# First stage of a two-layer transformer kernel: projections of the feed-forward part moved next to the normalisation of queries and keys, their product given to GpSimd

## The chip, the cores and the metric

The kernel runs on one core of a Trainium2 chip. The core has a matrix engine (TensorE, PE in the profile, with its weight loads shown as PEld), a vector engine (VectorE, DVE), a scalar engine (ScalarE, ACT), GpSimd (POOL) and SyncE (SP), which here only issues transfers. The engines run their own instruction streams and meet at semaphores. The metric is the device time of one execution in microseconds, as the median of several; lower is better.

## The reference, cut to what matters

Two transformer layers over one sequence of 2048 tokens of width 128, everything in float32:

```
xn = layernorm(x)
x = x + attn0(xn) + ffn0(xn)           # layer 0
xn = layernorm(x)
x = x + attn1(xn) + ffn1(xn)           # layer 1

attn0: q, k, v = split(xn @ w_qkv.T + b_qkv); 16 heads of 8 dims
       q = q / |q|, k = k / |k|        # norm of each head's 8 numbers
       score = (1 + arccos(q.k)) ** -3.2, scaled by row and column sums, rows normalised
       out = probs @ v @ w_out.T + b_out
ffn0:  gate = xn @ (w_gate/127).T; up = xn @ (w_up/127).T      # 384 columns each
       out = (silu(gate) * up) @ (w_down/127).T                # back to 128
```

The change touches only the stage that computes the first layernorm, q, k and v, the norms of q and k, and all of ffn0.

## The kernel before

The program runs stage after stage, each a block of five instruction streams that ends with all engines meeting: `stage_project0` (this change), `stage_attention0` (16 heads), `stage_project1`, `stage_attention1`, `stage_output`. Within a stage the order on each engine is the order in which the code is written; nothing reorders it.

`stage_project0` holds the 2048 tokens as 16 tiles of 128 (NT = 16) or as four chunks of 512 columns (NCH = 4), and the 384 hidden columns of ffn0 as three tiles of 128 (M0 = 3), so that gate and up have 12 pieces each, of 128x512, numbered k.

- **TensorE** turns the normalised x (L245), multiplies it with the weights of q, k, v (L252), then does gate and up piece by piece (L261 into `psG`, L263 into `psU`, two PSUM banks each, k % 2). Piece k waits for the product of piece k - 2. After all twelve it turns q and k, split into three bfloat16 parts (L271, 96 transposes into `psT`), and at last does the down projection (L279, 16 tiles of three matmuls into `psQ`).
- **VectorE** does layernorm, adds the bias to q, k and v, and then works on q and k as one array of 128x4096: squares (L174, into the array `two`), sums in groups of 8 (L176), waits for a square root from ScalarE, one Newton step and the reciprocal (L178 to L183 on 128x512), the scaling (L186, `qkn_ready`), and the split into three bfloat16 parts (L189 to L192, `parts_ready`). Only after that come its twelve products of gate and up (L198, one input in PSUM, one in SBUF) and its sixteen additions of down and x into `base` (L203).
- **ScalarE** copies the turned x, takes the square root of the norms (L224), does twelve Silu (L229 into `sil`, two buffers), then copies twelve pieces of turned parts from PSUM (L233 into `stg`).
- **GpSimd** waits for `qkn_ready`, and makes the products of pairs of q and of k that head 0 needs (`products`: a copy at L287, eight multiplications at L294; `factors`: L305 to L312).
- **SyncE** stores six pieces of `stg` as they come (L127), waits for them, waits for all of `base`, stores it (L131) and waits for that store.

The stage ends when every engine has come to its end. `stage_attention0` uses the memory of `base` as a scratch array (`folds`, first written by VectorE at L527, some way into head 0) and loads `base` again at its end.

Of the kernel before, what the change touches and what calls it, by code (L numbers as in the profile page):

```python
# [6 lines left out]
ALU = mybir.AluOpType  # L7
# [21 lines left out]
KST = NPART * NPART * HD0  # L29
GEXP = -3.2  # L30
# [29 lines left out]
def stage_project0(nc, io, sb):  # L60
# [3 lines left out]
    with ExitStack() as ctx:  # L64
# [29 lines left out]
        sil = t("sil0", [P, 2, BANK])  # L94
# [13 lines left out]
        gate_ps, up_ps, sil_ready, h_ready = sem("gate_ps0"), sem("up_ps0"), sem("sil_ready0"), sem("h_ready0")  # L108
        pt_ps, pt_ready, parts_stored = sem("pt_ps"), sem("pt_ready"), sem("parts_stored")
        down_ps, base_ready, base_stored = sem("down_ps0"), sem("base_ready0"), sem("base_stored")  # L110
        qkn_ready, mono, mono_ready = sem("qkn_ready"), sb["mono"], sb["mono_ready"]
        psTb = psT[:, :, :].rearrange("p a b -> p (a b)").bitcast(BF16).rearrange("p (a b) -> p a b", a=2)

        with nc.Block() as block:
            @block.sync
            def _(sp):
# [7 lines left out]
                for i in range(NPART):  # L124
                    for x in range(2):
                        sp.wait_ge(pt_ready, 2 * (2 * i + x) + 2)
                        sp.dma_start(io["parts"][i, x].rearrange("h d t -> (h d) t"), stg[:, i, x, :])\  # L127
                          .then_inc(parts_stored, 16)
                sp.wait_ge(parts_stored, 16 * 2 * NPART)
                sp.wait_ge(base_ready, NT)  # L130
                sp.dma_start(io["base"], base[:, :, :].rearrange("p n d -> p (n d)")).then_inc(base_stored, 16)  # L131
                sp.wait_ge(base_stored, 16)

            @block.vector
            def _(eng):
# [53 lines left out]
                link(eng.tensor_copy(parts[:, 0, :, :], qkn[:, :, :]))  # L189
                link(eng.tensor_tensor(qk[:, :, :], qkn[:, :, :], parts[:, 0, :, :], ALU.subtract))  # L190
                link(eng.tensor_copy(parts[:, 1, :, :], qk[:, :, :]))
                eng.tensor_tensor(parts[:, 2, :, :], qk[:, :, :], parts[:, 1, :, :], ALU.subtract)\  # L192
                   .then_inc(parts_ready, 1)
                for k in range(NCH * M0):
                    n_, m = k // M0, k % M0
                    eng.wait_ge(up_ps, k + 1)
                    eng.wait_ge(sil_ready, k + 1)
                    eng.scalar_tensor_tensor(out=hT[:, m, n_ * BANK:(n_ + 1) * BANK], in0=psU[:, k % 2, :],  # L198
                                             scalar=DEQ, in1=sil[:, k % 2, :], op0=ALU.mult,
                                             op1=ALU.mult).then_inc(h_ready, 1)  # L200
                for k in range(NT):
                    eng.wait_ge(down_ps, k + 1)
                    eng.scalar_tensor_tensor(out=base[:, k, :], in0=psQ[:, k % 2, 0:D], scalar=DEQ,  # L203
                                             in1=x_in[:, k, :], op0=ALU.mult, op1=ALU.add).then_inc(base_ready, 1)

            @block.gpsimd
            def _(eng):
                fac = sb["fac"]
                for i, f in enumerate(F_ROWS):
                    eng.memset(fac[:, 0, :, 3 * NMON + i:3 * NMON + i + 1], GQK * GQK)  # L210
                    eng.memset(fac[:, 1, :, 3 * NMON + i:3 * NMON + i + 1], -f * GQK * GQK)
                eng.wait_ge(qkn_ready, 1)
# [4 lines left out]
            def _(eng):  # L217
# [5 lines left out]
                eng.wait_ge(n2_ready, 1)  # L223
                eng.activation(nrm[:, :], n2[:, :], ACT.Sqrt).then_inc(nrm_ready, 1)  # L224
                for k in range(NCH * M0):
                    eng.wait_ge(gate_ps, k + 1)
                    if k >= 2:
                        eng.wait_ge(h_ready, k - 1)
                    eng.activation(sil[:, k % 2, :], psG[:, k % 2, :], ACT.Silu, scale=DEQ).then_inc(sil_ready, 1)  # L229
                for k in range(2 * NPART * 2):  # L230
# [6 lines left out]
            def _(eng):  # L237
# [17 lines left out]
                for k in range(NCH * M0):  # L255
                    n_, m = k // M0, k % M0
                    rhs = xnT[:, n_ * BANK:(n_ + 1) * BANK]
                    if k >= 2:
                        eng.wait_ge(sil_ready, k - 1)
                        eng.wait_ge(h_ready, k - 1)  # L260
# [4 lines left out]
                eng.wait_ge(parts_ready, 1)  # L265
                for k in range(2 * NPART * 2):
# [1411 lines left out]
```

## Time and profile before

| | |
|---|---|
| median of 3 runs | 3647.53 us (3646.39 to 3648.2) |
| the profiled execution | 3644.35 us, its span 3642.6 us |
| busy shares of the span | PE 86%, ACT 83%, DVE 77%, POOL 73% |
| first stage | up to 116.07 us after the span's start |
| layer 0's attention | from there to about 1940 us |

The profile is of one execution. Its rows tell for a line, an engine and an operation how many instructions there were, how long they took and what ended the idle time before them. In the timeline a row starts with the start in microseconds and the duration of the group of instructions; of a group of several, the duration runs from the start of the first to the end of the last. A tile name stands for the memory and not for the variable: `two` is the array that the code of the first stage calls `qkn`.

### The profile page before, as it was taken

To read this page: it belongs to the slowest core of one execution; us is meant where nothing else is said; L and a number is where in the kernel's file an instruction comes from. 1 tells how busy PE (TensorE), PEld (TensorE's weight loads), DVE (VectorE), ACT (ScalarE), POOL (GpSimd) and SP (SyncE) were. 2 spreads that over 40 slices of the span, in tenths; PEclk is the share of its full clock that TensorE was granted. 3 is DMA by queue.
4 is the path that set the end of the run, shared out by engine and by line. 5 is a ranking of instruction groups with operands and counts; after the bars stand their busy time and mean duration, and the time that the engine had idled before them with its cause. 6 is when DMAs were issued, how large, how long until landed. Compare 5 with 4: busy or idle time off the path is not lost. (4 is left out here: it accounts for less than half of the span.)

```text
span 3642.6 us, 59779 instructions
## 1 busy us (share of the span) xinstructions
PE 3123.6 (86%) x19264; PEld 1306.7 (36%) x19264; DVE 2800.0 (77%) x3981; ACT 3013.6 (83%) x2658; POOL 2666.2 (73%) x1450
## 2 busy tenths in 40 slices
PE   4888888888889888898886968888888888888899
PEld 2322222222222122221222424555555555555547
DVE  7678988889888898888987977787877778787301
ACT  1799999999999999999995846887878878788722
POOL 2698988989889898898973525776777777677600
PEclk8876677766777667776676978999999999999999
DMA  0100000000000000000001450110001110000100
GB/s 23 53 7 7 0 7 7 6 7 0 6 7 6 6 0 6 7 6 6 0 10 38 140 163 25 42 30 25 24 25 34 34 30 24 25 24 27 38 0 12
DMA packets 59508, 85.46 MB, mean 23 GB/s; under 512 B 9808, under 2 KB 45904, under 8 KB 58960
## 3 DMA queue, kind: packets, MB, share of 16 engines
q1 hardware_dynamic: 59344, 83.06, 8.1%
q8 instruction: 129, 2.11, 0.2%
q14 instruction: 35, 0.29, 0.0%
HBM read 52.44 MB, written 30.54 MB: 23 GB/s over the span
## 5 line engine op out<-in xcount | busy, mean ns | idle before, releaser
L1195 POOL TENSOR_TENSOR lo<-pr,hi 128x1024 f16<-128x1024 f32 x384 | 917.3, 2413 | 384.5 <-ACT hi L1321 382.5
L1244 DVE TENSOR_REDUCE mx<-mx_ps 128x1 f32<-128x512 f32 x1024 | 659.8, 683 | 165.3 <-PE mx_ps L1359 161.8
L1336 ACT ACTIVATE pr<-s_ps 128x1024 f32<-128x1024 f32 x512 | 532.3, 1040 | 264.4 <-PE s_ps L1380 235.2
L1321 ACT ACTIVATE hi<-pr 128x1024 f16<-128x1024 f32 x512 | 548.2, 1072 | 0.0
L1359 PE MATMUL mx_ps<-ka,qa 128*128 128x512 f16 x1024 | 385.8, 398 | 141.5 <-DVE mx L1244 116.9
L671 ACT ACTIVATE wt<-wt 128x2048 f32<-128x2048 f32 x256 | 485.0, 1896 | 0.5
L477 POOL TENSOR_TENSOR wt<-base,wt 128x1024 f32<-128x1024 f32 x192 | 459.1, 2391 | 15.1
L662 ACT ACTIVATE wt<-wt,theta_bias 128x10240 f32<-128x10240 f32 (+2 forms) x96 | 464.3, 4837 | 0.9
L1399 PE MATMUL pv_ps<-vh,hi 128*128 128x129 f16 x4096 | 432.9, 222 | 11.2 <-ACT sums L1327 5.8
L1378 PE MATMUL s_ps<-qa,ka 128*128 128x512 f16 x1024 | 396.7, 387 | 35.1 <-issue 22.4
L473 POOL TENSOR_TENSOR base<-base,shift 128x1024 f32<-128x1024 f32 x192 | 364.1, 1897 | 83.7 <-DVE base L527 83.7
L1399 PE MATMUL pv_ps<-vh,lo 128*128 128x65 f16 x4096 | 418.6, 194 | 0.0
L1380 PE MATMUL s_ps<-qb,kb 65*128 65x512 f16 x1024 | 397.7, 388 | 0.0
L1399 PEld LDWEIGHTS pv_ps<-vh,hi 128*128 128x128 f16 x4096 | 372.8, 98 | 62.4 <-POOL lo L1195 11.1
L477 POOL TENSOR_TENSOR wt<-vb,wt 128x1024 f32<-128x1024 f32 x160 | 379.2, 2370 | 12.6
L1399 PEld LDWEIGHTS pv_ps<-vh,lo 128*128 128x128 f16 x4096 | 366.4, 99 | 55.7 <-issue 3.3
L750 PE MATMUL m_ps<-mst 110*128 110x512 f16 (+1 forms) x640 | 321.2, 609 | 47.5 <-ACT wt L651 19.6
L643 ACT ACTIVATE wt<-m_ps 128x1024 f32<-128x1024 f32 x352 | 332.9, 1032 | 24.8 <-PE m_ps L719 23.2
L473 POOL TENSOR_TENSOR vb<-vb,shift 128x1024 f32<-128x1024 f32 x160 | 303.4, 1897 | 60.1 <-DVE vb L527 60.1
L750 PE MATMUL r_ps<-mst 111*128 111x512 f16 (+1 forms) x768 | 314.5, 445 | 35.0 <-DVE wt L515 10.2
L1195 DVE TENSOR_TENSOR lo<-pr,hi 128x1024 f16<-128x1024 f32 x128 | 261.7, 2045 | 86.9 <-ACT hi L1321 86.9
L719 PE MATMUL m_ps<-mst 109*128 109x512 f16 x1024 | 307.6, 385 | 21.6 <-ACT wt L643 10.7
(196 smaller groups left out, 5265.4 us busy)
## 6 DMA issues: line engine op xcount, KB each, us to landing
qk<-stg SPq DMA_DIRECT2D x6, 2048.0 KB, 11.0
vh<-v SPq DMA_DIRECT2D x16, 520.0 KB, 3.5
qa<-qk SPq DMA_DIRECT2D x16, 512.0 KB, 3.6
ka<-qk SPq DMA_DIRECT2D x32, 256.0 KB, 4.7
v<-v_st SPq DMA_DIRECT2D x3, 2080.0 KB, 8.0
qst<-parts_dram SPq DMA_DIRECT2D x144, 32.0 KB
kst<-parts_dram SPq DMA_DIRECT2D x144, 32.0 KB
qk<-stg SPq DMA_DIRECT2D x4, 1024.0 KB, 8.2
```

What stands on the lines that cost most here:

```text
L473: eng.tensor_tensor(v, v, shift[:, 0:1].to_broadcast([P, 2 * BANK]), ALU.subtract)\
L477: eng.tensor_tensor(u, v, u, ALU.mult).then_inc(cubic, 1)
L662: eng.activation(wt[:, k:k + many, :], wt[:, k:k + many, :], ACT.Ln, bias=theta_bias[:, 0:1], scale=-2.0 if k >= NQ else -KA / (G4 * G4 * ...
L671: eng.activation(wt[:, k, :], wt[:, k, :], ACT.Exp, scale=GEXP, accum_out=n_c[:, k:k + 1])\
L750: mm = eng.matmul(slot(r)[:, cols(i, BANK)], mst[0:rows, 1, cols(k)], mst[0:rows, 0, rhs], start=True, stop=True)
L1195: eng.tensor_tensor(lo[:, i % NHL, :, :], pr_slot(i), hi[:, i % NHL, :, :], ALU.subtract).then_inc(lo_done, 1)
L1244: eng.tensor_reduce(mx4[:, q // NCH, q % NCH:q % NCH + 1], mx_ps[:, q % 2, :], AX.X, ALU.max)\
L1321: eng.activation(hi[:, i % NHL, :, :], pr_slot(i), ACT.Copy).then_inc(hi_done, 1)
L1336: eng.activation(pr_slot(i), s_ps[:, i % 2, :, :], ACT.Exp, scale=SM).then_inc(exp_done, 1)
L1378: eng.matmul(s_ps[:, i % 2, n_, :], ka[:, par, k * P:(k + 1) * P], qa[:, par, w], start=True, stop=False)
L1380: mm = eng.matmul(s_ps[:, i % 2, n_, :], kb[0:HD1 + 1, par, k * P:(k + 1) * P], qb[0:HD1 + 1, par, w], start=False, stop=True)
L1399: mm = eng.matmul(pv_ps[:, j // 2, j % 2 * OW:j % 2 * OW + cols], half[:, i % NHL, n_, j * P:(j + 1) * P], vh[:, par, k, 0:cols], start=(k ...
```

## The change

Five things change, all but the last in `stage_project0`.

- ScalarE now copies the up projection out of PSUM too, scaled, into a new buffer `up` (right behind each Silu), and a piece of PSUM is free for TensorE as soon as that copy is done (`up_taken`), not when the product is.
- The twelve products of gate and up go from VectorE to GpSimd, ahead of GpSimd's work on head 0. Both inputs are then in SBUF.
- ScalarE's square root of the norms comes behind four of the twelve pieces (NRM = 4).
- TensorE does the first half of down, turns the first part of q and k, does the second half of down, and turns the other two parts. VectorE announces each part for itself. Down goes into `psG` and `psU`, four token tiles to a bank, and VectorE adds x to four tiles with one instruction.
- SyncE issues the store of `base` ahead of its wait for the six part stores and doesn't wait for the store of `base` in this stage. VectorE waits for it (`base_stored`) in `stage_attention0` before its head 0.

```diff
@@ SyncE
-                sp.wait_ge(parts_stored, 16 * 2 * NPART)
-                sp.wait_ge(base_ready, NT)
+                sp.wait_ge(base_ready, NCH)
                 sp.dma_start(io["base"], base[:, :, :].rearrange("p n d -> p (n d)")).then_inc(base_stored, 16)
-                sp.wait_ge(base_stored, 16)
+                sp.wait_ge(parts_stored, 16 * 2 * NPART)
@@ VectorE
-                link(eng.tensor_copy(parts[:, 0, :, :], qkn[:, :, :]))
+                eng.tensor_copy(parts[:, 0, :, :], qkn[:, :, :]).then_inc(parts_ready, 1)
+                eng.wait_ge(parts_ready, 1)
...
-                for k in range(NCH * M0):
-                    n_, m = k // M0, k % M0
-                    eng.wait_ge(up_ps, k + 1)
-                    eng.wait_ge(sil_ready, k + 1)
-                    eng.scalar_tensor_tensor(out=hT[:, m, n_ * BANK:(n_ + 1) * BANK], in0=psU[:, k % 2, :],
-                                             scalar=DEQ, in1=sil[:, k % 2, :], op0=ALU.mult,
-                                             op1=ALU.mult).then_inc(h_ready, 1)
-                for k in range(NT):
-                    eng.wait_ge(down_ps, k + 1)
-                    eng.scalar_tensor_tensor(out=base[:, k, :], in0=psQ[:, k % 2, 0:D], scalar=DEQ,
-                                             in1=x_in[:, k, :], op0=ALU.mult, op1=ALU.add).then_inc(base_ready, 1)
+                for c in range(NCH):
+                    eng.wait_ge(down_ps, 4 * c + 4)
+                    four = slice(4 * c, 4 * c + 4)
+                    eng.scalar_tensor_tensor(out=base[:, four, :], in0=down(c).rearrange("p (n d) -> p n d", d=D),
+                                             scalar=DEQ, in1=x_in[:, four, :], op0=ALU.mult,
+                                             op1=ALU.add).then_inc(base_ready, 1)
@@ GpSimd
+                for k in range(NCH * M0):
+                    n_, m = k // M0, k % M0
+                    eng.wait_ge(up_taken, k + 1)
+                    eng.tensor_tensor(hT[:, m, n_ * BANK:(n_ + 1) * BANK], sil[:, k % 2, :], up[:, k % 2, :],
+                                      ALU.mult).then_inc(h_ready, 1)
                 eng.wait_ge(qkn_ready, 1)
@@ ScalarE
-                eng.wait_ge(n2_ready, 1)
-                eng.activation(nrm[:, :], n2[:, :], ACT.Sqrt).then_inc(nrm_ready, 1)
                 for k in range(NCH * M0):
+                    if k == NRM:
+                        eng.wait_ge(n2_ready, 1)
+                        eng.activation(nrm[:, :], n2[:, :], ACT.Sqrt).then_inc(nrm_ready, 1)
                     eng.wait_ge(gate_ps, k + 1)
                     if k >= 2:
                         eng.wait_ge(h_ready, k - 1)
                     eng.activation(sil[:, k % 2, :], psG[:, k % 2, :], ACT.Silu, scale=DEQ).then_inc(sil_ready, 1)
+                    eng.wait_ge(up_ps, k + 1)
+                    eng.activation(up[:, k % 2, :], psU[:, k % 2, :], ACT.Copy, scale=DEQ).then_inc(up_taken, 1)
@@ TensorE
                     if k >= 2:
-                        eng.wait_ge(sil_ready, k - 1)
-                        eng.wait_ge(h_ready, k - 1)
+                        eng.wait_ge(up_taken, k - 1)
...
+                for k in range(NT // 2):
+                    project_down(k)
+                turn_part(0)
+                for k in range(NT // 2, NT):
+                    project_down(k)
+                for i in range(1, NPART):
+                    turn_part(i)
@@ stage_attention0, VectorE
                 for x in range(2):
                     stack(0, x)
+                eng.wait_ge(sb["base_stored"], 16)
                 head(0, first=True)
```

TensorE, from the last piece of gate and up to the first matmul of the next stage. Before, all 96 transposes of the parts (L271) and then the 48 matmuls of down (L279):

```order
L261 MATMUL psG<-xnT,wg 128x512
L263 MATMUL psU<-xnT,wu 128x512
L271 MATMUL psT<-ident_b,parts 128x128 x96
L279 MATMUL psQ<-wd,hT 128x128 x48
L114 UNCONDITIONAL_BRANCH
```

And now, where `psG` and `psU` take the two halves of down:

```order
L270 MATMUL psG<-xnT,wg 128x512
L272 MATMUL psU<-xnT,wu 128x512
L293 MATMUL psG<-wd,hT 128x128 x24
L282 MATMUL psT<-ident_b,parts 128x128 x32
L293 MATMUL psU<-wd,hT 128x128 x24
L282 MATMUL psT<-ident_b,parts 128x128 x64
L120 UNCONDITIONAL_BRANCH
```

One third of the transposes now stands between the halves of down, and the other two thirds close the stage.

ScalarE, from the copies of turned x to the copies of turned parts. Before:

```order
L222 ACTIVATE xnT<-psT 128x512 x4
L224 ACTIVATE nrm<-n 128x512
L229 ACT_TABLE_LOAD
L229 ACTIVATE sil<-psG 128x512 x12
L233 ACTIVATE stg<-psT 128x1024 x12
```

And now, from the third of the four pieces ahead of the square root to the first behind it (a piece is a pair of L237 and L239):

```order
9 L237 ACTIVATE sil<-psG 128x512
10 L239 ACTIVATE up<-psU 128x512
11 L237 ACTIVATE sil<-psG 128x512
12 L239 ACTIVATE up<-psU 128x512
13 L233 ACT_TABLE_LOAD
14 L233 ACTIVATE nrm<-n 128x512
15 L237 ACT_TABLE_LOAD
16 L237 ACTIVATE sil<-psG 128x512
17 L239 ACTIVATE up<-psU 128x512
```

The square root moved behind four pieces, and there are two table loads more.

## Rows read from the trace of the kernel before

**Rows 1.** Busy time by stretch: start:end, length, then each engine; PEclk, DMA

```profile
42.00:70.00 28.00, 0.00 (x0) 0.00 (x0) 27.43 (x12) 2.56 (x4) 14.06 (x4) 0.50 0.00 0
70.00:74.00 4.00, 3.28 (x4) 1.51 (x5) 1.17 (x2) 0.60 (x1) 3.92 (x9) 0.50 0.00 0
74.00:90.00 16.00, 16.00 (x38) 6.94 (x37) 6.21 (x9) 5.39 (x9) 5.12 (x7) 0.98 0.00 1
```

**Rows 2.** Timeline of VectorE from 32 to 75 us: start, duration, engine, line

```profile
32.65 4.42 DVE L174 TENSOR_TENSOR two<-qk 128x4096 f32<-128x4096 f32 x1
37.11 4.42 DVE L176 TENSOR_REDUCE n<-two 128x512 f32<-128x4096 f32 x1
...
42.69 3.35 DVE L179 RECIPROCAL ntmp<-nrm 128x512 f32<-128x512 f32 x1
46.07 0.69 DVE L180 TENSOR_TENSOR ntmp<-ntmp,n 128x512 f32<-128x512 f32 x1
...
55.83 2.29 DVE L189 CAST parts<-two 128x4096 bf16<-128x4096 f32 x1
58.16 4.50 DVE L190 TENSOR_TENSOR qk<-two,parts 128x4096 f32<-128x4096 f32 x1
62.69 2.58 DVE L191 CAST parts<-qk 128x4096 bf16<-128x4096 f32 x1
65.31 4.67 DVE L192 TENSOR_TENSOR parts<-qk,parts 128x4096 bf16<-128x4096 f32 x1
```

**Rows 3.** Timeline of TensorE and ScalarE: projections, square root, turning, down

```profile
31.80 1.02 PE L261 MATMUL psG<-xnT,wg 128*128 128x512 f32 x2
41.56 0.63 ACT L224 ACTIVATE nrm<-n 128x512 f32<-128x512 f32 x1 [22.58 <-DVE n L176]
42.21 1.28 ACT L229 ACT_TABLE_LOAD   x1
81.37 1.02 PE L261 MATMUL psG<-xnT,wg 128*128 128x512 f32 x2
82.43 0.60 ACT L229 ACTIVATE sil<-psG 128x512 f32<-128x512 f32 x1 [1.12 <-PE psG L261]
90.60 11.11 ACT L233 ACTIVATE stg<-psT 128x1024 bf16<-128x1024 bf16 x12 [0.71 <-PE psT L271]
100.39 10.94 PE L279 MATMUL psQ<-wd,hT 128*128 128x128 f32 x96
```

**Rows 4.** DMA issues up to 125 us: KB each, median us to landing

```profile
parts_dram<-stg SPq DMA_DIRECT2D x6, 512.0 KB, 2.6
base_dram<-base SPq DMA_DIRECT2D x1, 1024.0 KB, 3.8
```

**Rows 5.** Timeline: issue of the store of base, next stage's first instruction

```profile
111.74 0.33 SPq L131 DMA_DIRECT2D base_dram<-base  x1
116.07 0.06 DVE L494 MEMSET theta_bias<- 128x1 f32 x1 [4.42 <-PEq L114]
```

**Rows 6.** Timeline of GpSimd: head 0's products, and head 1's at 117.25

```profile
55.86 2.52 POOL L287 COPY mono_x<-two 128x256 f32<-128x256 f32 x1 [54.59 <-DVE two L186]
58.46 13.67 POOL L294 TENSOR_TENSOR mono_p<-mono_x 128x256 f32<-128x256 f32 x8
77.94 1.25 POOL L312 TENSOR_TENSOR fac<-mono_p,fac 128x576 f16<-128x576 f32 x1
117.25 3.37 POOL L294 TENSOR_TENSOR mono_p<-mono_x 128x256 f32<-128x256 f32 x8
```

**Rows 7.** One line's instructions: duration in ns, min/median/max

```profile
L1066 POOL TENSOR_TENSOR hl<-ra,hl x64: 1154/1160/1167, 2001.5 to 2133.2; 128x512 f16<-128x512 f32 x64
L477 POOL TENSOR_TENSOR wt<-base,wt x192: 2361/2390/2427, 131.6 to 1941.8; 128x1024 f32<-128x1024 f32 x192
L1195 DVE TENSOR_TENSOR lo<-pr,hi x128: 1202/2096/2703, 2216.6 to 3432.9; 128x1024 f16<-128x1024 f32 x128
```

**Rows 8.** Busy time by stretch, layer 0's attention: columns as in rows 1

```profile
630.00:1030.00 400.00, 352.70 (x1306) 84.96 (x1308) 341.57 (x447) 393.14 (x275) 363.67 (x213) 0.70 0.02 5
```

## What the change does to the time: the prediction

> **What bounds the kernel now.** I first read busy time by stretch. From 42 to 70 us TensorE does nothing, ScalarE is busy for 2.6 us of 28, and VectorE is busy for 27.4 [rows 1]: one engine carries the stage. The timeline of VectorE says with what: squares, sums, reciprocals and the split of q and k, one behind the other from 32.65 to 69.98 us [rows 2]. Only then come gate and up (TensorE full from 74 to 90 [rows 1]), the turning of the parts (12 copies, 11.1 us), down (10.9 us) [rows 3] and the store of base, issued at 111.74 and landed 3.8 us later [rows 4, 5]. The next stage starts at 116.07 [rows 5], 0.53 us behind the landing. So the stage is two chains laid end to end: VectorE's, 70 us, and then 46 us of ffn0, turning and storing. None of the second needs VectorE's chain but the turning. Everything behind 116 us is the same work in both kernels, so what the stage loses in length the whole should lose.
>
> **The change part by part.** I follow each engine through the new order with durations of the old one.
>
> *Price of a piece.* In the old loop ScalarE's Silu lasts 0.60 us and starts 1.06 us after its matmul (81.37 to 82.43); with the 1.12 us that it waits for TensorE that is 1.72 us for a pair of gate and up, 0.86 each [rows 3]. The copy of up is the same shape from the same memory: 0.60. GpSimd's product of 128x512 isn't in this stage; its nearest rows are 1.16 us for 128x512 with a half-precision output, and 2.39 us for a float32 product of 128x1024, or 1.2 for half of it [rows 7]. I take 1.16, with 1.2 as the other end: 12 x 0.04 = 0.5 us at most, nothing below.
>
> *What VectorE and GpSimd do to each other.* GpSimd's small copy of 128x256 lasted 2.52 us from 55.86, until 0.26 us after VectorE's cast ended (58.12), and its eight multiplications of 3.37 us lasted 13.67 us beside L190 to L192 [rows 6, 2]. One GpSimd instruction gets through at each border between two VectorE instructions. The reverse holds too: VectorE's L191 is 0.29 us longer than its like L189, L192 0.25 longer than 4.42, and far later, beside GpSimd products of 2.1 us, VectorE's product L1195 has a median of 2096 ns against a least of 1202 [rows 2, 7]. But beside VectorE's instructions with one input in PSUM, GpSimd's L477 stays within 2361 to 2427 ns [rows 7]. So who has two inputs in SBUF, or is a cast, waits for GpSimd's running instruction and then holds it up. No row shows a sum (L176) or a reciprocal (L179, L183) beside GpSimd; they have one input, so I take them as free, and price the contrary below. L178 and L182 (tensor with scalar) I count with the casts. The Trainium skill (SBUF — State Buffer, section Who interferes with whom) has the same rule: an exclusive lock held for the whole instruction, and a tensor_reduce that never takes it on this chip; by it the time is the 3617 of the sum below, and without it for sum and reciprocals it is B's 3626. It speaks against this change only in that each product on GpSimd may hold VectorE up.
>
> *The walk.* Piece 0: matmuls from 31.80 [rows 3], Silu 32.86, copy done at 34.3. GpSimd is locked out by L174 until 37.07; product 0 ends at 38.25. Silu 2 waits for it, so products 1 to 3 follow at 1.2 us beside the sum L176 and end at 39.5, 40.8 and 42.05; ScalarE has copied piece 3 at 40.85. Its table load (1.28 [rows 3]) ends at 42.15, the square root at 42.8 instead of 42.19: VectorE **+0.6**. Another table load, then pieces 4 on, the first Silu at 44.15. Product 4 runs beside L179 and ends at 46.6. VectorE takes L180 at 46.7; L181 has to wait for product 5, **+1.15**; L182 for product 6, **+1.2**; products 7 to 9 run beside the reciprocal L183, and L186 waits for the rest of 9, **+0.2**. Product 10, shut out by L186 (54.5 to 58.95), delays L189 by **1.15**, and product 11 delays L190 by **1.15**. Sum 5.45: VectorE's chain ends at 69.98 + 5.45 = **75.4**. The last product is done at 63.6.
>
> *GpSimd behind it.* Its copy for head 0 now comes at the border of L190 and L191 and its first multiplication at the next; one border less than before is left, so beyond L192 it has the old rest (72.13 - 69.98 = 2.15) and one multiplication of 0.55 more, and then the factors, from 72.13 to 79.19 before = 7.06 [rows 6]. 75.4 + 2.7 + 7.06 = **85.2 us**. Before this was hidden (79.2 against 115.5); now it is the last thing in the stage.
>
> *TensorE, ScalarE and stores.* Gate and up are through by 57.6 (ScalarE gives a piece each 1.2 to 1.7 us behind TensorE), half of down takes 10.94 / 2 = 5.5 [rows 3] and ends at 63.1, part 0 (there since VectorE's cast, 62.4) is turned in 4 x 0.93 = 3.7 and done at 66.8, the other half of down at 72.3, part 1 (there at 70.6) at 76.0, part 2 (there at 75.4) at 79.7. Its store lands 2.6 us later [rows 4], 82.3, three before GpSimd. VectorE's four additions follow L192 and end at about 78.3. The store of base is issued behind the last part's, near 80, and lands at 84; VectorE asks for it only before head 0, eight us into the next stage: nothing, and if that cover went, 3.8 us at most. The two loads of tables are inside the walk. Sixteen additions become four: off the path. The next stage's stack loads (SyncE, ahead of nothing but themselves) shift with the stage.
>
> *Sum.* Next stage's first instruction: 85.2 + 0.5 = 85.7, against 116.07: **-30.4 us**. The profiled execution would be 3644.35 - 30.4 = 3614.0; the runs have a median 3.2 higher than it, so **3617.1 us**, a ratio of 0.9917.
>
> **The rivals.**
>
> *A. VectorE isn't held up by GpSimd* (it wins every border, or a product lets go early). Then its chain ends at 69.98 + 0.6, and GpSimd, if it has kept its place, at about 79.8: -35.8, **3611.7**. Against it stand the 2096 ns of L1195; for it, that the observed delays in this very stage are only 0.1 to 0.3 us, because the GpSimd instructions there were short.
>
> *B. Sum and reciprocals lock as well.* Every product then waits for a border. Walking it the same way, product 3 ends at 46.3, the square root at 47.0, one product of 1.2 goes into each of the borders up to L191, L192 ends at 83.8, and GpSimd at 83.8 + 3.4 + 7.06 = 94.3: -21.3, **3626**. This is also the case in which the change only half does what it says.
>
> *C. TensorE falls to its low clock.* With no matmul from 42 to 70 the granted clock was 0.50 (1.2 of 2.4 GHz), and stayed there for the first 4 us of work [rows 1]. Now TensorE works with gaps, in pieces paced by ScalarE and GpSimd. In layer 0's attention, also work with gaps, the granted clock is 0.70 on average with TensorE busy for 353 of 400 us [rows 8]. At 0.70 a pair takes 2.4 us: pieces 6 to 11 from 45.5 end at 60, half of down at 67.7, part 0 at 71.4, down at 79, parts 1 and 2 at 86.5, landed 89.2, stage end 89.7: -26.4, **3621**. At 0.50 all through (pairs 3.4, down 21.9) the same walk gives 102.1, or 3633.5. The Trainium skill (TensorE: Matmul & The Clock Gate, section A second HAM failure mode: psum-queue depth-cycling) describes a kernel in which short idles between groups of matmuls on PSUM banks make the clock go up and down: that is this rival. Against it: matmuls from 74 to 90 and the turning behind them had gaps and a full clock.
>
> *D. Slower than before.* Only the work behind the stage could eat 30 us, and there only ScalarE's stage of 16 heads is long enough (1826 us, 116.07 to 1941.8 [rows 5, 7]). There ScalarE is busy for 393 of 400 us and TensorE for 353 at a clock of 0.70 [rows 8]. TensorE becomes the bound when its clock falls under 0.70 x 353 / 400 = 0.62 on average, and from there each further 1% costs 18 us; 30 us are lost at 0.61. For that, a denser first stage would have to change what the chip grants over the next 1.8 ms. Price: **3648** or more. Nothing in the rows ties the two, since the clock in the attention stage starts from an idle gap of 5 us in both kernels.
>
> **How the numbers follow.** The walk as written: 55% (between 3613 and 3621, since each of five borders can fall the other way by about 1 us, and 1.16 or 1.2 us is open). A 15%, B 10%, C 15% (most of it near 3621), D 2%, and 3% for what I don't see, in either direction. The range from **3610 to 3627** takes in the walk, A, B and C at 0.70, and leaves out C at 0.50, D and the unseen. A change of 0.2% (7.3 us) is about what a measurement of this kernel can tell from none; all but D and part of the unseen lie beyond it: faster 96%, same 2%, slower 2%.
>
> **What the profile of the changed kernel would show.** The next stage's first memset at 84 to 88 us, with GpSimd's last factors (7 us of them, alone) ending half a microsecond before it and the part stores landed before. L174's like at 32.65 with the first product ending 1.2 us behind it; VectorE's small instructions between the two reciprocals 1.2 us apart more than before; casts and L186's like starting about 1 us late. The sum and the two reciprocals with products at 1.2 us inside them: if these are 3 to 4 us long, B holds. A granted clock near 1.0 from 45 to 80 us; near 0.5 or 0.7 with the last part store as the end of the stage, C. VectorE's chain ending by 71, A. The forecast is wrong altogether if layer 0's attention, from 116.07 to the start of the last L477 at 1941.8 [rows 7], isn't within 3 us of these 1825.7.

## The result, and the profile after

| | before | changed |
|---|---|---|
| median of the runs | 3646.96 us (3642.92 to 3648.2, 4 runs) | 3615.33 us (3613.58 to 3623.75, 4 runs) |
| ratio, 95% interval | | 0.9923 [0.9906, 0.9939] |
| the profiled execution, its span | 3644.35, 3642.6 us | 3623.75, 3621.9 us |
| next stage's first instruction | 116.07 us | 84.81 us |

The medians lie 31.6 us apart; the forecast was 30.4, and 3617.1 us for the median. The profiled execution of the changed kernel is the slowest of its four, which matters below.

The timeline of VectorE in the changed kernel, from the squares on, to be laid beside [rows 2]. A row starts with start and duration in microseconds:

```profile
32.62 4.42 DVE L179 TENSOR_TENSOR two<-qk 128x4096 f32<-128x4096 f32 x1
37.08 4.42 DVE L181 TENSOR_REDUCE n<-two 128x512 f32<-128x4096 f32 x1
42.56 0.43 DVE L183 TENSOR_SCALAR nrm<-nrm 128x512 f32<-128x512 f32 x1 [1.06 <-ACT nrm L233]
43.02 3.35 DVE L184 RECIPROCAL ntmp<-nrm 128x512 f32<-128x512 f32 x1
46.41 1.65 DVE L185 TENSOR_TENSOR ntmp<-ntmp,n 128x512 f32<-128x512 f32 x1
48.09 1.64 DVE L186 TENSOR_TENSOR ntmp<-ntmp,nrm 128x512 f32<-128x512 f32 x1
49.76 1.38 DVE L187 TENSOR_SCALAR ntmp<-ntmp 128x512 f32<-128x512 f32 x1
51.17 3.35 DVE L188 RECIPROCAL nrm<-ntmp 128x512 f32<-128x512 f32 x1
54.56 5.53 DVE L191 TENSOR_TENSOR two<-qk,nrm 128x4096 f32<-128x4096 f32 x1
60.12 3.24 DVE L194 CAST parts<-two 128x4096 bf16<-128x4096 f32 x1
63.40 4.50 DVE L196 TENSOR_TENSOR qk<-two,parts 128x4096 f32<-128x4096 f32 x1
...
70.56 4.66 DVE L199 TENSOR_TENSOR parts<-qk,parts 128x4096 bf16<-128x4096 f32 x1
```

The sum L181 and the two reciprocals last as long as before. L185, L186, L187, L191 and L194 are each 0.95 to 1.1 us longer than their likes before (0.69, 0.69, 0.43, 4.42, 2.29). With the root 0.37 us late that makes 5.3 us, and the chain ends at 75.22 instead of 69.98.

GpSimd in the same stretch, to be laid beside [rows 6]:

```profile
34.36 7.58 POOL L217 TENSOR_TENSOR hT<-sil,up 128x512 f32<-128x512 f32 x4 [33.09 <-ACT up L239]
45.00 2.50 POOL L217 TENSOR_TENSOR hT<-sil,up 128x512 f32<-128x512 f32 x2 [3.06 <-ACT up L239]
47.67 1.51 POOL L217 TENSOR_TENSOR hT<-sil,up 128x512 f32<-128x512 f32 x1 [0.17 <-ACT up L239]
49.39 1.47 POOL L217 TENSOR_TENSOR hT<-sil,up 128x512 f32<-128x512 f32 x1 [0.21 <-ACT up L239]
...
56.26 4.96 POOL L217 TENSOR_TENSOR hT<-sil,up 128x512 f32<-128x512 f32 x1 [0.45 <-ACT up L239]
61.17 2.46 POOL L309 COPY mono_x<-two 128x256 f32<-128x256 f32 x1
63.70 13.67 POOL L316 TENSOR_TENSOR mono_p<-mono_x 128x256 f32<-128x256 f32 x8
...
83.18 1.25 POOL L334 TENSOR_TENSOR fac<-mono_p,fac 128x576 f16<-128x576 f32 x1
```

The last product (56.26, 4.96 us) shows how the two engines shut each other out: it was ready before L191 ended, was held until it did (60.1), was through at 61.2, and L194 waited for it. GpSimd ends at 84.43, the next stage begins 0.38 us later. The part stores had landed before that: the last was issued at 80.1 and took 2.6 us, so 82.7.

What the rest gave back. Layer 0's attention took 1824.5 us by the count of the prediction (84.81 to the last L499 at 1909.3), against 1825.7. But layer 1's attention, from the first to the last product of GpSimd (L1195 before, L1218 now), took 1239.2 us against 1225.8. That is where 31.3 us of stage became 20.7 us of span: 31.3, and 1.2 in layer 0's attention, and 1.6 between the two attention stages, less 13.4. Busy time by stretch, the changed kernel (start:end, length, PE, PEld, DVE, ACT, POOL, then TensorE's granted clock):

```profile
2173.20:3412.40 1239.20, 1075.19 (x11155) 671.41 (x11153) 948.17 (x1307) 1015.57 (x1084) 913.74 (x384) 0.97 0.10 27
```

and the kernel before:

```profile
2207.30:3433.10 1225.80, 1066.02 (x11154) 667.96 (x11152) 948.66 (x1307) 1015.60 (x1084) 914.20 (x384) 0.98 0.10 27
```

Every engine but TensorE was busy for the same time; TensorE 9.2 us longer, at a granted clock of 0.97 instead of 0.98. Whether that is chance or a consequence was the first question of the experiments.

### The profile page after: what moved, and what is told of

Same layout as the page of the kernel before. It is cut to its first block and busy times, and to the rows that moved or that the text cites. A ratio compares the mean times of both kernels' runs of the same rounds, so it can differ in the third digit from the quotient of the medians.

```text
span 3621.9 us, 59761 instructions
## 1 busy us (share of the span) xinstructions
PE 3124.6 (86%) x19264; PEld 1305.9 (36%) x19264; DVE 2793.6 (77%) x3957; ACT 3023.0 (83%) x2672; POOL 2688.0 (74%) x1462
## 5 line engine op out<-in xcount | busy, mean ns | idle before, releaser
L1218 POOL TENSOR_TENSOR lo<-pr,hi 128x1024 f16<-128x1024 f32 x384 | 916.9, 2412 | 398.7 <-ACT hi L1344 395.1
L499 POOL TENSOR_TENSOR wt<-base,wt 128x1024 f32<-128x1024 f32 x192 | 459.5, 2393 | 15.0
L499 POOL TENSOR_TENSOR wt<-vb,wt 128x1024 f32<-128x1024 f32 x160 | 379.2, 2370 | 12.5
L1218 DVE TENSOR_TENSOR lo<-pr,hi 128x1024 f16<-128x1024 f32 x128 | 261.2, 2040 | 86.7 <-ACT hi L1344 86.7
```

Source lines behind the costliest of these rows:

```text
L499: eng.tensor_tensor(u, v, u, ALU.mult).then_inc(cubic, 1)
L1218: eng.tensor_tensor(lo[:, i % NHL, :, :], pr_slot(i), hi[:, i % NHL, :, :], ALU.subtract).then_inc(lo_done, 1)
```

## The experiments

To compare stages I count from the start of the squares (the first 128x4096 instruction of VectorE) to the next stage's first instruction, since that start lies anywhere between 31.55 and 32.65 us in the profiles. Before: 83.4 us, changed kernel: 52.2.

### The same two kernels once more

No edit. 

> The changed kernel once more, unchanged. In its profile the stretch of layer 1's attention between the first and the last product L1218 had taken 1239.2 us against 1225.8 before, 13.4 us longer, with a granted clock of 0.91 to 0.95 in some stretches of 100 us. Theory 1, chance of the execution: the stretch comes out anywhere between 1226 and 1240 us in this profile, the times of the runs spread over some 10 us, and the median is 30 to 33 us under that of the kernel before (ratio 0.991 to 0.9925). Theory 2, tied to the change: the stretch is again at 1238 or more, and the gain in the total stays near 20 us.

Measured: 3615.1 us (3610.93 to 3618.31, 5 runs) against 3644.67 (3639.27 to 3648.8, 16 runs), ratio 0.9916 [0.9903, 0.993]. Layer 1's stretch took 1229.6 us, between the two values.

> The kernel before once more, unchanged, for a second profile of layer 1's attention (first to last product L1195). Theory 1, chance: the stretch lies anywhere between 1226 and 1240 us. Theory 2, tied to the change: it is 1226 to 1228 us again. The first stage must end at 116.1 us as in the first profile, within 0.3.

Measured: 3640.21 us, layer 1's stretch 1226.0, next stage at 114.78, not within 0.3 of 116.1. The squares start 0.76 us earlier: 0.1 of that is the landing of x (VectorE's first instruction at 7.42 instead of 7.54), the rest the 32 matmuls of q, k and v, which ran in 13.2 us instead of 13.8. The count from the squares is 82.9 against 83.4; here the granted clock was back from 0.50 about 1 us sooner, once gate and up went on behind VectorE's chain.

So 9.6 of the 13.4 us of the first profile were that execution's own, and the medians differ by 29.6 us where the stage gives 27 to 31. What is left of it comes at the end.

The repeat of the changed kernel showed something else. Its stage took 56.1 us instead of 52.2 (31.65 to 87.70), although GpSimd was through at 84.2. Its VectorE:

```profile
45.43 1.63 DVE L185 TENSOR_TENSOR ntmp<-ntmp,n 128x512 f32<-128x512 f32 x1
47.10 0.69 DVE L186 TENSOR_TENSOR ntmp<-ntmp,nrm 128x512 f32<-128x512 f32 x1
47.83 1.37 DVE L187 TENSOR_SCALAR ntmp<-ntmp 128x512 f32<-128x512 f32 x1
```

its TensorE and clock before that (timeline, then busy time by stretch, the granted clock third from the end):

```profile
44.00 1.13 PE L270 MATMUL psG<-xnT,wg 128*128 128x512 f32 x2 [1.87 <-ACT up L239]
44.97 1.71 PE L272 MATMUL psU<-xnT,wu 128*128 128x512 f32 x2
46.46 1.91 PE L270 MATMUL psG<-xnT,wg 128*128 128x512 f32 x2
```

```profile
44.00:46.00 2.00, 2.00 (x4) 1.01 (x5) 1.97 (x2) 1.53 (x3) 1.97 (x2) 0.79 0.00 0
46.00:48.00 2.00, 2.00 (x3) 0.67 (x2) 1.93 (x3) 0.60 (x1) 1.13 (x2) 0.50 0.00 0
```

and its GpSimd, ScalarE and TensorE later, then the first profile's row for the same half of down, and the clock at that place:

```profile
53.55 13.64 POOL L217 TENSOR_TENSOR hT<-sil,up 128x512 f32<-128x512 f32 x3 [0.45 <-ACT up L239]
58.59 0.60 ACT L237 ACTIVATE sil<-psG 128x512 f32<-128x512 f32 x1 [3.41 <-POOL hT L217]
59.73 8.43 PE L293 MATMUL psG<-wd,hT 128*128 128x128 f32 x48 [3.46 <-ACT up L239]
56.23 5.62 PE L293 MATMUL psG<-wd,hT 128*128 128x128 f32 x48 [0.69 <-ACT up L239]
```

```profile
58.00:60.00 2.00, 0.27 (x1) 0.27 (x2) 2.00 (x1) 1.09 (x2) 2.00 (x2) 0.70 0.00 0
60.00:62.00 2.00, 2.00 (x10) 2.00 (x11) 1.97 (x2) 0.00 (x0) 2.00 (x2) 0.50 0.00 0
```

Read in order: while ScalarE loads tables for the root, TensorE stands for 1.9 us; in this execution its clock then fell to 0.50 (1.2 of 2.4 GHz) for about 3 us, piece 6 came 0.7 us late, its product missed the border at L186 (0.69 us, nobody in the way), and three products were left for the borders behind the long instruction L191, where the first profile had one. There one goes through per border, so three products took 13.64 us. The last Silu needs a buffer that the product two pieces back must free: it waited 3.41 us. Down waits for all copies of up, and the turning of all parts and their stores stand behind down.

So TensorE stood a second time, for 3.46 us, and its clock fell a second time: it was 0.50 from about 59 to 65.6 us, and the first half of down took 8.43 us instead of 5.62. Everything behind down moves with it, and GpSimd, through at 84.2, would have allowed an end at 84.6. So these 2.8 us make up most of the 3.9 us that the stage was longer; by an estimate from these rows 1.1 us are left for the late start of down itself. This is rival C on a small scale: the first fall acts through GpSimd, and the second lengthens down directly.

### One part alone: parts turned as they come

```diff
 # before.py, TensorE: between the second and third piece of gate and up
+                    if k == 2:
+                        for q in range(2 * NPART * 2):
+                            i, x, g = q // 4, q // 2 % 2, q % 2
+                            if q % 4 == 0:
+                                eng.wait_ge(parts_ready, i + 1)
...
-                eng.wait_ge(parts_ready, 1)
-                for k in range(2 * NPART * 2):
```

> One part alone on the kernel before: the parts are turned one by one as VectorE makes them, between the second and the third piece of gate and up; all else as before. Theory (the stage was two chains end to end): the last part is turned by 73.7 us, gate and up then run from there to 91, down to 102, the store of base lands at 106.3, and the next stage starts at 106.8 instead of 116.07, so 9 us less and a time of 3637 to 3639 us. Rival (turning was worth nothing since TensorE is bound elsewhere): next stage still at 113 us or later.

Measured: next stage at 107.03, stage count 75.1, which is 7.8 less than the 82.9 of the repeat of before (9.3 expected); 3633.77 us (10 runs), ratio 0.9973 [0.9964, 0.9982]. The rival is out. The median is 10.9 us lower than that of the kernel before, and under the 3637 to 3639 expected; by the interval it is 7 to 13 us lower, which takes in the 7.8 of the stage.

### The projections alone

```diff
 # after.py
-                for k in range(NT // 2):
-                    project_down(k)
-                turn_part(0)
-                for k in range(NT // 2, NT):
-                    project_down(k)
-                for i in range(1, NPART):
-                    turn_part(i)
+                eng.wait_ge(parts_ready, NPART)
+                for i in range(NPART):
+                    turn_part(i)
+                for k in range(NT):
+                    project_down(k)
...
                 sp.wait_ge(parts_stored, 16 * 2 * NPART)
+                sp.wait_ge(base_stored, 16)
```

> The changed kernel with the other two parts undone: turning waits for all three parts and comes ahead of all of down, and the store of base is awaited in the stage. Theory: VectorE's chain ends at 75.1 as in the changed kernel, turning at 86.6, down at 97.6, the store lands at 101.8, next stage at 102.3; 17.5 us more than the changed kernel (84.8), 13.8 less than before; 3632 to 3635 us. Together with the run that only turns early it tells whether the gain of the two parts adds up (9.3 + 13.8 = 23.1 of 31.3) or whether they need each other. Rival (the projections alone bring it all): next stage at 90 us or less.

Measured: next stage at 102.58 (102.3 expected), stage count 70.3; 3630.46 us (5 runs; 3632 to 3635 expected), ratio 0.996 [0.9946, 0.9973]. So the two parts alone save 7.8 and 12.6 us, 20.4 together, and the change 26.8 to 30.7 by the same count, of which 0.9 is the store of base (next run). They need each other: turned early alone, gate, up and down still run behind VectorE's chain; projected early alone, turning and down do.

### The store of base awaited in the stage

```diff
                 sp.wait_ge(parts_stored, 16 * 2 * NPART)
+                sp.wait_ge(base_stored, 16)
```

> The changed kernel with the store of base awaited in the first stage again, as before (the store still issued ahead of the wait for the parts). In the changed kernel that store lands at 85.1 us and GpSimd ends at 84.4. Theory: the next stage starts at 85.6 to 85.7, 0.9 us later than in the changed kernel; the awaited store was worth no more than that because GpSimd's factors end at nearly the same time. Rival (the late wait is worth a whole store): 88.5 or more.

Measured: stage count 53.05, 0.9 us more than 52.2, as expected. The time of its single run was 3610.21 us.

### The products cut to 8 columns

```diff
-                    eng.tensor_tensor(hT[:, m, n_ * BANK:(n_ + 1) * BANK], sil[:, k % 2, :], up[:, k % 2, :],
+                    eng.tensor_tensor(hT[:, m, n_ * BANK:n_ * BANK + 8], sil[:, k % 2, 0:8], up[:, k % 2, 0:8],
                                       ALU.mult).then_inc(h_ready, 1)
```

> The changed kernel, but each of GpSimd's twelve products of gate and up covers 8 of its 512 columns; the others are set to 0 at the start, so the feed-forward part of layer 0 is left out. Theory (a GpSimd instruction holds VectorE up for its whole length): L185 and L186 are back at 0.69 us each, L187 at 0.43, L191 at 4.4, L194 at 2.3; the chain to L199 ends at 70.0 to 70.6 instead of 75.2, GpSimd's factors at 79.3 to 79.8, next stage at 79.9 to 80.3. Rival (VectorE is late because of the square root behind four pieces, or because of memory traffic of ScalarE and TensorE): the chain ends at 74 us or later all the same.

Measured: 3615.97 us (single run). VectorE's timeline:

```profile
45.61 0.69 DVE L185 TENSOR_TENSOR ntmp<-ntmp,n 128x512 f32<-128x512 f32 x1
46.33 0.69 DVE L186 TENSOR_TENSOR ntmp<-ntmp,nrm 128x512 f32<-128x512 f32 x1
47.06 0.43 DVE L187 TENSOR_SCALAR ntmp<-ntmp 128x512 f32<-128x512 f32 x1
...
50.91 4.42 DVE L191 TENSOR_TENSOR two<-qk,nrm 128x4096 f32<-128x4096 f32 x1
55.37 2.33 DVE L194 CAST parts<-two 128x4096 bf16<-128x4096 f32 x1
```

The chain ended at 69.69. All five delays are gone with the length of GpSimd's instructions (L194 keeps 0.04 us), and the rival is out. But the next stage came at 81.80, not 80: GpSimd ended at 78.9, and SyncE had issued the last part store only at 79.0; with its 2.6 us that is the end. TensorE's and ScalarE's own chain (half of down, part 0, half of down, two parts) stood right behind GpSimd. It began late even here: GpSimd's instructions took 0.20 us alone, but two of them took 3.53 us beside L191, and the last Silu waited 1.82 us for a buffer. The size of a GpSimd instruction doesn't help it to get past a long one.

### A memset in place of the product

```diff
-                    eng.tensor_tensor(hT[:, m, n_ * BANK:(n_ + 1) * BANK], sil[:, k % 2, :], up[:, k % 2, :],
-                                      ALU.mult).then_inc(h_ready, 1)
+                    eng.memset(hT[:, m, n_ * BANK:(n_ + 1) * BANK], 1.0).then_inc(h_ready, 1)
```

> The changed kernel with each of the twelve products replaced by a memset of the same 128x512 (the feed-forward part of layer 0 is left out). GpSimd then writes as much, and reads nothing. Theory 1 (VectorE and GpSimd meet at reads only where VectorE has two inputs in SBUF): L185, L186 at 0.69 and L191 at 4.42 us, unchanged by GpSimd, while the cast L194 and L187 may be late by up to one memset; chain end at 70 to 71.5. Theory 2 (any GpSimd instruction holds up any of these): L185, L186 and L191 are each late by most of a memset's length (0.3 to 0.6 us).

Measured: 3615.13 us (single run), chain end at 69.58, a little under the expected 70 to 71.5. GpSimd's and VectorE's timelines:

```profile
51.63 0.53 POOL L217 MEMSET hT<- 128x512 f32 x1 [1.19 <-ACT up L238]
53.34 0.53 POOL L217 MEMSET hT<- 128x512 f32 x1 [1.19 <-ACT up L238]
55.06 0.53 POOL L217 MEMSET hT<- 128x512 f32 x1 [1.19 <-ACT up L238]
```

```profile
50.70 4.42 DVE L191 TENSOR_TENSOR two<-qk,nrm 128x4096 f32<-128x4096 f32 x1
55.16 2.57 DVE L194 CAST parts<-two 128x4096 bf16<-128x4096 f32 x1
```

Two memsets ran their 0.53 us in the middle of L191, which has two inputs in SBUF, and neither felt the other. The cast L194 ended 0.28 us late, held by the third; L187 (0.60 us) ended 0.17 us late. Theory 1 holds: an instruction with two inputs meets GpSimd at reads only, a cast at writes too. The Trainium skill (SBUF — State Buffer, section Who interferes with whom) says that a VectorE instruction with two SBUF inputs contends with a GpSimd instruction that reads SBUF, not with one that only writes it, and that casts and tensor_scalar can take the whole shared pair of ports. The traces agree, with 0.53 us for a memset against the 4.96 of a product in the same place.

### The root ahead of all pieces

```diff
-NRM = 4
+NRM = 0
```

> The changed kernel with ScalarE's square root of the norms ahead of all pieces (NRM = 0) instead of behind four. Theory: ScalarE has to stand until VectorE's sums are there (41.5), so the pieces start at 43.5 and run to about 64 at 1.72 us each; VectorE gets its root 0.35 us earlier but is held up at more borders (about 8 us), TensorE turns part 0 only behind half of down at 76, and is last: part stores land near 92, next stage at 90 to 93, 5 to 8 us later than the changed kernel. Rival (the place of the root is worth 0.4 us only, since the rest hides): next stage at 84 to 85.5.

Measured: next stage at 105.43, stage count 73.5, 21 us more than the changed kernel where I expected 5 to 8; 3635.94 us. GpSimd and TensorE:

```profile
52.69 26.05 POOL L217 TENSOR_TENSOR hT<-sil,up 128x512 f32<-128x512 f32 x8 [0.45 <-ACT up L239]
67.55 2.08 PE L270 MATMUL psG<-xnT,wg 128*128 128x512 f32 x2 [3.42 <-ACT up L239]
77.44 8.43 PE L293 MATMUL psG<-wd,hT 128*128 128x128 f32 x48 [3.45 <-ACT up L239]
```

The direction was right, the size wrong by a factor of three. Four pieces that come late fall into the long instructions: eight products took 26.05 us there, and with two buffers ScalarE and TensorE go at that pace too. What I hadn't counted at all is the clock. TensorE first stood for 9.26 us and then for 3.42 and 3.45 us; behind each of these the granted clock was 0.50, and the first half of down took 8.43 us instead of 5.62. How the 21 us divide between the borders and the clock isn't shown. What NRM = 4 buys is four products beside or just ahead of the free sum, and a TensorE that goes on working.

### Factors shared, root behind three pieces

```diff
-NRM = 4
+NRM = 3
...
+                for at in (0, 2 * NMON):
+                    last = eng.tensor_copy(fac[:, 0, :, at:at + NMON], pr[:, 0, :, :])
+                link(last)
+                link(eng.tensor_tensor(fac[:, 0, :, NMON:2 * NMON], pr[:, 0, :, :], fac[:, 0, :, 0:NMON],
+                                       ALU.subtract))
```

> The changed kernel with the factors of head 0 shared: GpSimd makes those of k, VectorE those of q behind its last addition to base; and the root behind three pieces instead of four. Theory (GpSimd's factors end the stage): the chain ends 0 to 0.4 us earlier, GpSimd at 82.0 to 82.4, and now the part stores (82.7) end the stage: next stage at 82.8 to 83.3, 1.5 to 2 us earlier than the changed kernel. Rival (something else than GpSimd ends the stage): next stage within 0.3 of 84.8. In the total that is 0.05%, under what the runs can tell.

Measured: stage count 51.6, 0.6 less than 52.2, where 1.5 to 2 were expected; 3618.55 us (5 runs), ratio 0.9932 [0.9919, 0.9946]. With the root one piece earlier, two products instead of one came behind L191 (8.24 us for both), and GpSimd began its factors 0.9 us later by the count. Its remaining factors then met VectorE's, which cost another 1.1 us:

```profile
55.12 8.24 POOL L224 TENSOR_TENSOR hT<-sil,up 128x512 f32<-128x512 f32 x2 [0.45 <-ACT up L246]
...
77.53 1.21 POOL L334 TENSOR_TENSOR fac<-mono_p 128x448 f16<-128x448 f32 x1
78.69 0.54 POOL L335 CAST fac<-mono_p 128x128 f16<-128x128 f32 x1
79.17 1.47 POOL L334 TENSOR_TENSOR fac<-mono_p 128x448 f16<-128x448 f32 x1
```

The last three take 0.94, 0.32 and 0.94 us alone; GpSimd ended at 83.1 and still ended the stage. In the total the runs can't tell this kernel from the changed one.

### Products in halves

```diff
+                    for q in range(2):
+                        part = slice(n_ * BANK + q * BANK // 2, n_ * BANK + (q + 1) * BANK // 2)
+                        half = slice(q * BANK // 2, (q + 1) * BANK // 2)
+                        ins = eng.tensor_tensor(hT[:, m, part], sil[:, k % 2, half], up[:, k % 2, half], ALU.mult)
```

> The changed kernel with each product of gate and up on GpSimd as two instructions of 128x256. Theory (what VectorE waits for is the one running instruction): L185, L186, L187, L191 and L194 are each late by at most 0.6 us instead of 0.95 to 1.1, but more of them are; the chain ends at 73 to 74.5 instead of 75.2, while the last product is done later than 61.2. Rival (VectorE waits until GpSimd's queue of ready instructions is empty): the delays at L185 to L187 stay at 0.95 or more.

Measured: 3622.79 us (single run). The delays of VectorE halved (L185 1.23, L186 1.10, L187 0.97 us), its chain ended at 72.5, and the stage was 10.6 us longer, 62.8. GpSimd:

```profile
52.31 22.16 POOL L220 TENSOR_TENSOR hT<-sil,up 128x256 f32<-128x256 f32 x8 [0.31 <-ACT up L242]
```

The theory for VectorE's chain holds, and so does its number, if one counts that the squares began 0.8 us earlier than in the first profile. What I had not asked is who pays: a border lets one instruction through, whatever its size, so halves need twice the borders; the last product came at 74.5, down began at 66.7. Not all of the 10.6 us is the price of halves, though. This execution also had the low clock from 44 to 49 us (0.81, 0.50, 0.84), as the repeat of the changed kernel had, and against that one's 56.1 us the stage is 6.7 us longer. Behind a stand of 9.98 us the clock was at 0.50 again, and the first half of down took 8.38 us.

### Four buffers

```diff
-        sil, up = t("sil0", [P, 2, BANK]), t("up0", [P, 2, BANK])
+        sil, up = t("sil0", [P, NB, BANK]), t("up0", [P, NB, BANK])
...
-                    if k >= 2:
-                        eng.wait_ge(h_ready, k - 1)
+                    if k >= NB:
+                        eng.wait_ge(h_ready, k - NB + 1)
```

> The changed kernel with four buffers each for ScalarE's two outputs (sil and up) instead of two, so that a Silu waits for the product four pieces back. From the start of the squares (L179) to the next stage's first instruction the first profile of the changed kernel took 52.2 us, the second 56.1; in the second a product of GpSimd missed its turn at L186, the next ones got through one by one at later borders, Silu 11 waited 3.4 us for a product, and down, turning and stores came that much later. Theory (the two buffers carry GpSimd's lateness to ScalarE and TensorE): with four no Silu waits for a product in the end, the last copy of up is done some 24 us after the start of the squares, and the stage takes 51.5 to 53.5 us by that count, whichever way the borders fall. Rival (down itself waits for the late products): 55 or more again when a product is late.

Measured: stage count 51.8, the last copy of up done 23.2 us behind the start of the squares; 3615.55 us (4 runs), ratio 0.992 [0.9903, 0.9936]. The borders fell as in the first profile, though, so this run alone doesn't decide between theory and rival. The next does.

> Four buffers, and the factors of head 0 shared between GpSimd (k) and VectorE (q), root behind four pieces. Theory: neither GpSimd's tail nor a late product ends the stage, only TensorE's and ScalarE's chain of down and turning; by the count from the squares 50 to 51.8 us against 52.2 and 56.1 of the changed kernel and 83.4 before. In the total 0 to 5 us under the changed kernel, so a ratio to the kernel before of 0.990 to 0.992. Rival (sharing brings new waits of the two engines for each other): 53 or more.

The edits are those of the two runs above, the root behind four pieces. In this execution the clock fell (0.50 from 46 to 48 us) and the product missed its border, as in the repeat of the changed kernel:

```profile
53.09 13.64 POOL L225 TENSOR_TENSOR hT<-sil,up 128x512 f32<-128x512 f32 x3 [0.45 <-ACT up L247]
54.99 0.60 ACT L245 ACTIVATE sil<-psG 128x512 f32<-128x512 f32 x1 [0.26 <-PE psG L278]
56.50 5.62 PE L301 MATMUL psG<-wd,hT 128*128 128x128 f32 x48 [0.69 <-ACT up L247]
```

The same 13.64 us for three products, but the last Silu waits only for its matmul, TensorE stands for 0.69 us instead of 3.46 and keeps its clock, down takes 5.62 us instead of 8.43, and the stage took 51.1 us where the changed kernel took 56.1. That shows how a late product reaches the end of the stage: through the two buffers, and through the clock that falls while TensorE waits. Of the 5.0 us some 1.5 belong to the shared factors (GpSimd needs 5.6 us for its factors instead of 7), so the two edits aren't separated by this run. GpSimd's tail still ended the stage (82.28, next stage at 82.66), against the theory. The median is 3613.04 us (3608.36 to 3617.3, 4 runs), ratio to before 0.9912 [0.9896, 0.9929]. It is the lowest median of the kernels with several runs, but within the interval of the changed kernel; the gain of 1 to 5 us is shown in the stage, not in the total.

### What stays open

All fourteen profiles have layer 1's attention. In the five kernels or repeats in which SyncE awaits the store of base within the first stage (both of before, turning alone, projections alone, store awaited) the stretch took 1225.6 to 1226.8 us. In the nine others it took 1228.9 to 1239.2. The store itself is long done by then; of the engines' busy times only TensorE's differs (1064.9 to 1066.5 against 1066.5 to 1075.2). That doesn't explain the split, because at its edge the busy times are equal: 1066.5 us in the run with the store awaited (stretch 1226.8), and 1066.5 and 1066.6 in the run with factors shared and the repeat (1229.2 and 1229.6). Theory 2 as I had put it is out, since the repeat gave 1229.6 and the run with the store awaited, otherwise the changed kernel, 1226.8. But chance alone is a poor word for a split as clean as this, and one pair of kernels that differ in only this wait is too little to call it the cause. The cause stays open; it is worth 2 to 14 us, as much as several of the edits tried here.

## Why the prediction was right, point by point

**What bounds the kernel** held: VectorE's chain and then ffn0, laid end to end. Each of the two halves of the remedy alone brought less than both.

**The walk** came out near for the stage: 85.7 for the next stage's start, measured 84.81. Its terms: VectorE's chain 75.4, measured 75.22; its delay 5.45, measured 5.3; GpSimd's end 85.2, measured 84.43; the part stores 82.3, landed at 82.7. Inside the sum three terms were placed wrongly. I had L181's like (L186) and L182's like (L187) delayed but not L180's like (L185), only 0.2 at L186's like (L191), and 1.15 at L190's like (L196) that didn't come; measured were 0.96, 0.95, 0.95, 1.11 and 0.95 at L185, L186, L187, L191 and L194, and nothing at L196 (4.50 in both). The errors cancelled, which is luck. The product took 1.27 us, longer than the 1.16 and 1.2 of the bounds (12 x 0.11 = 1.3 us, not 0.5 at most), and the last one ended at 61.2, not 63.6. Who is first at a border is decided by tenths of a microsecond that such a walk doesn't have. That the median came within 2 us of 3617.1 is in part luck too: the stage was 52.2 us in one execution and 56.1 in another of the same kernel, and layer 1's attention took 4 to 13 us more than before, which the sum doesn't have.

**The term that the repeat shows too small** is the one I put at nothing: that a late product only shifts GpSimd's tail. Through the two buffers it also shifts down, turning and stores, and the wait lets TensorE's clock fall, which makes down 2.8 us longer; in the repeat the two together were 3.9 us, in the run with the root first they are part of the 21. I had walked TensorE's side with a margin of three microseconds and not asked what the margin hung on.

**The rivals.** A (VectorE not held up) is refuted by the 0.95 us five times over, and by the run with tiny products, where the delays vanish. B (sums and reciprocals lock as well) is refuted by L184 and L188 at 3.35 us with products of 1.27 us beside them. C (low clock) was right as a mechanism and wrong in size: not an average over the stage but, in the repeat, two falls to 0.50, one of some 3 us behind the stand of 1.9 us around the root and one of some 7 us behind the stand of 3.5 us ahead of down, paid with 3.9 us together; in the first profile none. D (slower, by a lower clock in layer 0's attention) didn't happen: that stage took 1824.5 us against 1825.7. The place where the clock did move was layer 1's attention, which I hadn't named.

**The awaited store** was put at nothing, and is worth 0.9 us and not a whole store, because GpSimd ends nearly as late.

## What to carry to other kernels

When VectorE and GpSimd are made to work side by side on data in SBUF, count borders and not only busy time: one GpSimd instruction passes between two VectorE instructions that lock, so long VectorE instructions set GpSimd's pace, and cutting the same GpSimd work into more instructions makes it worse for whoever waits for GpSimd. Put such work beside instructions that don't lock (here the sum and the reciprocals), and give it enough buffers that its lateness stays its own: here the lateness cost most where it let TensorE stand until its clock fell. And when one profile of a changed kernel is told from one of the kernel before, look at the stage that changed: here the spans said 20.7 us, the stage 31.3, and the medians agreed with the stage.

## What the runs showed of the hardware

- A GpSimd product of 128x512 with both inputs in SBUF took 1.27 us alone and up to 4.96 us behind a VectorE instruction with two inputs in SBUF; a GpSimd memset of the same size took 0.53 us with or without it.
- TensorE stood for 1.9 to 3.2 us around the root. Behind stands of 1.86, 1.86, 2.39 and 3.22 us (the first profile, the store awaited, four buffers, factors shared) the granted clock stayed at 1.00; behind 1.87, 2.00 and 2.38 us (the repeat, the halves, the last run) it fell to 0.50 for some 3 us. Among these the length of the stand doesn't tell which. Behind the longer stands ahead of down or between pieces, 3.42, 3.45 and 3.46 us (the root first, twice, and the repeat) and 9.98 us (the halves), it was 0.50 each time; where half of down followed, that took 8.4 us instead of 5.6.
- The store of base, 1 MB, landed 3.8 us after issue alone, and 4.7 to 5.2 us when issued 0.3 us behind the last part store.
